# A selective scan with its kept state moved from the scan's start operand into the first column of its input

## The reference

```python
x = x + dilation_3x3(_gn(x))
x = x + mamba_block(_gn(x))
x = x + conv_3x3(_gn(x)) + bias
x = x + conv_3x3(_gn(x)) + bias
```

```python
def step(h, inputs):
    dt_t, x_t, B_t, C_t = inputs
    h = h * jnp.exp(dt_t[..., None] * A) + (dt_t * x_t)[..., None] * B_t[:, None, :]
    y = jnp.einsum('bds,bs->bd', h, C_t)
    return (h, y)
```

## Time and profile before

| | |
|---|---|
| median of 3 runs | 15620.45 us |
| the profiled execution | 15622.6 us, span 15620.4 us |
| DVE busy | 14588.6 us, 93% |
| POOL busy | 13980.9 us, 90% |
| PE busy | 12518.6 us, 80% |
| ACT busy | 8590.8 us, 55% |
| mean granted TensorE clock | 0.916 |

### The profile page before, as it was taken

One profiled execution on the slowest core, in us unless ns is written; L12 is line 12 of the kernel. 1 busy time (PEld: TensorE's weight loads), 2 busy tenths in 40 slices (PEclk: granted clock), 3 DMA queues, 4 the chain that ended last, 5 costly groups with the idle time before them and its releaser, 6 DMA issues.

```text
span 15620.4 us, 161058 instructions
## 1 busy us (share of the span) xinstructions
PE 12518.6 (80%) x26824; PEld 4912.5 (31%) x26824; DVE 14588.6 (93%) x13134; ACT 8590.8 (55%) x15334; POOL 13980.9 (90%) x6232
## 2 busy tenths in 40 slices
PE   4888878887887887878878788887888888788786
PEld 1333333333333333333333333333333333333332
DVE  6999999999999999999999999999999999999996
ACT  3555555555555555555555555555555555555553
POOL 5989989899898998989989898998989999899895
PEclk9999989999999898999999899999999999999898
DMA  3343433433434343343433434343343333434333
GB/s 95 103 115 107 109 114 102 122 103 106 116 104 120 100 109 115 105 118 104 110 115 105 117 103 116 107 109 114 102 122 103 106 117 105 120 101 109 116 103 84
DMA packets 1248863, 1701.30 MB, mean 109 GB/s; under 512 B 399212, under 2 KB 548148, under 8 KB 1245428
## 3 DMA queue, kind: packets, MB, share of 16 engines
q1 hardware_dynamic: 1247700, 1689.55, 38.6%
HBM read 1525.54 MB, written 124.13 MB: 106 GB/s over the span
## 4 chain that ended last, share of the span: by engine, by line
DVE 26%; issue 26%; POOL 20%; PE 19%; SPq 4%; DMA 3%; ACT 1%; DVEq 1%; POOLq 1%; ACTq 0%
POOL hc L646 15%; DVE h L1167 13%; PE y_ps L947 12%; DVE u_in L1151 8%; POOL u_in L621 3%; PE proj_ps L903 3%; DMA c_sb<-bc_dram 2%; SPq L431 1%; SPq L499 1%; PE b_ps L995 1%; PE side_ps L934 1%; DVE stats L1042 1%; PE side_ps L958 1%; DVEq L1165 1%; DVE norm L1122 1%
## 5 line engine op out<-in xcount | busy, mean ns | idle before, releaser
L646 POOL TENSOR_TENSOR hc<-h,c_sb 128x1024 f32<-128x1024 f32 x4096 | 9781.5, 2400 | 1182.8 <-DVE h L1167 696.7
L947 PE MATMUL y_ps<-hc,ident 128*128 128x512 f32 x16400 | 8584.4, 653 | 1013.0 <-POOL hc L646 1006.4
L1167 DVE TENSOR_TENSOR_SCAN h<-a_ps,carry,u_in 128x512 f32<-128x512 f32 x7168 | 8798.9, 1264 | 390.4 <-POOL hc L646 253.1
L751 ACT ACTIVATE a_ps<-dt,a_neg 128x512 f32<-128x512 f32 x8192 | 5605.2, 689 | 6147.0 <-DVE h L1167 6129.7
L947 PEld LDWEIGHTS y_ps<-hc,ident 128*128 128x128 f32 x16400 | 3276.4, 207 | 4849.4 <-issue 3119.9
L1151 DVE TENSOR_TENSOR u_in<-dtx,b_ps 128x1024 f32<-128x1024 f32 x2816 | 3364.0, 1195 | 142.1 <-PE b_ps L995 116.3
L621 POOL TENSOR_TENSOR u_in<-dtx,b_sb 128x1024 f32<-128x1024 f32 x1281 | 3088.3, 2411 | 0.1
L995 PE MATMUL b_ps<-b_parts,select 96*128 96x512 bf16 x2816 | 1156.0, 411 | 1493.6 <-DVE u_in L1151 1484.9
L1167 DVE TENSOR_TENSOR_SCAN h<-a_ps,u_in 128x512 f32<-128x512 f32 x1024 | 1205.5, 1204 | 208.9 <-POOL hc L646 184.4
L995 PEld LDWEIGHTS b_ps<-b_parts,select 96*128 96x128 bf16 x2816 | 283.5, 101 | 3104.2 <-DVE u_in L1151 2611.7
L958 PE MATMUL side_ps<-padded,w_main 128*128 128x512 f32 x1632 | 894.3, 634 | 154.2 <-DVE z L1134 71.7
(11 more groups left out here) (99 smaller groups left out, 6671.0 us busy)
## 6 DMA issues: line engine op xcount, KB each, us to landing
c_sb<-bc_dram SPq DMA_DIRECT2D x4100, 256.0 KB, 3.2
b_sb<-bc_dram SPq DMA_DIRECT2D x1283, 256.0 KB, 3.2
raw<-x SPq DMA_DIRECT2D x17, 2048.0 KB
x_dram<-vmax SPq DMA_DIRECT2D x68, 512.0 KB, 4.7
x<-x_dram SPq DMA_DIRECT2D x136, 256.0 KB, 8.0
z<-x_dram SPq DMA_DIRECT2D x68, 512.0 KB, 8.3
out<-raw SPq DMA_DIRECT2D x272, 128.0 KB
x_dram<-x SPq DMA_DIRECT2D x129, 256.0 KB, 3.8
```

Of the source, the lines that this page charges most:

```text
L646: pool.tensor_tensor(hc[:, ring_at(c * S + s, HC_RING)], h[:, ring_at(c * S + s, H_RING)], c_sb[:, s // C_GROUP % C_RING, s % C_GROUP:s % ...
L751: act.activation(a_ps[:, a_slot(c * S + s, half)], dt[:, c % 2, half], ACT.Exp, scale=a_neg[:, at:at + 1]).then_inc(a_made, 1)
L947: mm = pe.matmul(y_ps[:, half], ident[:, :], hc[:, ring_at((c * S + s) % (NC * S), HC_RING), half], start=False, stop=(s == S - 1), skip_g ...
L1167: dve.tensor_tensor_scan(h[:, r, half], a_ps[:, a_slot(c * S + s, half)], u_in[:, s % U_RING, half], start, ALU.mult, ALU.add).then_inc(h_ ...
```

## The change

All scans start from the constant zero. Since h[0] = a[0] h_kept + u[0], the same result comes out when a[0] h_kept is first added into column 0 of u_in. Three things are done for it.

1. At the start of each chunk but the first, ACT computes `first_a`, the decays of the chunk's first token for all 32 states (two activations of 128 x 32), after a wait for its own last decay.
2. Between the decay of half 0 and that of half 1 of every state of those chunks, ACT runs `add_carry`: two activations on one column, Identity with scale = carry and bias = u_in's first column, written in place. It waits for the product (u_in by DVE or by POOL), and signals `carried`, for which the scan of half 0 now waits instead of the product.
3. DVE makes its product two states ahead instead of one: in state s, between the two scans, that for s + 2. Two products stand ahead of the loop's body for an image instead of one. In PE's queue the place of the broadcasts is as before. The third place of the convolutions begins at state 29 instead of 28, and the mean and variance of one norm ("z1") move by one state.

```diff
-PLACES = ((15, 16, 19, 22), (24, 25, 26, 27), (28, 30, S + 2, S + 2))
+PLACES = ((15, 16, 19, 22), (24, 25, 26, 27), (29, 30, S + 2, S + 2))
...
-MEAN_AT = {"joint": (0, 23), "z1": (3, 29), "x1": (6, 24)}
-VAR_AT = {"joint": (0, 27), "z1": (4, 0), "x1": (6, 27)}
+MEAN_AT = {"joint": (0, 23), "z1": (3, 30), "x1": (6, 24)}
+VAR_AT = {"joint": (0, 27), "z1": (4, 1), "x1": (6, 27)}
...
+        first_a = sb("first_a", [P, NH, S])
...
             def make_decay(b, c, s):
                 if s == 0:
                     act.wait_ge(dt_done, chunk(b, c, NH))
+                    if c:
+                        act.wait_ge(a_made, state(b, c - 1, S - 1, NH))
+                        for half in range(NH):
+                            first = act.activation(first_a[:, half, :], a_neg[:, half * S:(half + 1) * S], ACT.Exp,
+                                                   scale=dt[:, c % 2, half, 0:1])
+                        first.then_inc(first_done, 1)
                 for half in range(NH):
 
                     act.wait_ge(h_done, a_free(b, c, s, half))
                     at = half * S + s
                     act.activation(a_ps[:, a_slot(c * S + s, half)], dt[:, c % 2, half], ACT.Exp,
                                    scale=a_neg[:, at:at + 1]).then_inc(a_made, 1)
+                    if c and half == 0:
+                        add_carry(b, c, s)
+
+            def add_carry(b, c, s):
+
+                if s == 0:
+                    act.wait_ge(first_done, first_chunk(b, c))
+                if s in DVE_U:
+                    act.wait_ge(u_made, made_by_vector(b, c, s))
+                else:
+                    act.wait_ge(pu_made, made_by_pool(b, pool_index(c, s)))
+                for half in range(NH):
+                    u0 = u_in[:, s % U_RING, half, 0:1]
+                    made = act.activation(u0, first_a[:, half, s:s + 1], ACT.Identity, bias=u0,
+                                          scale=carry[:, half, s:s + 1])
+                made.then_inc(carried, 1)
...
-                    if s in DVE_U:
+                    if c:
+                        dve.wait_ge(carried, carried_state(b, c, s))
+                    elif s in DVE_U:
                         dve.wait_ge(u_made, made_by_vector(b, c, s))
                     else:
                         dve.wait_ge(pu_made, made_by_pool(b, pool_index(c, s)))
                 dve.wait_ge(a_made, state(b, c, s, NH) - (NH - 1 - half))
-                start = carry[:, half, s:s + 1] if c else 0.0
-                dve.tensor_tensor_scan(h[:, r, half], a_ps[:, a_slot(c * S + s, half)], u_in[:, s % U_RING, half], start,
+                dve.tensor_tensor_scan(h[:, r, half], a_ps[:, a_slot(c * S + s, half)], u_in[:, s % U_RING, half], 0.0,
                                        ALU.mult, ALU.add).then_inc(h_done, 1)
...
-                if 0 in DVE_U:
-                    make_u(b, 0, 0)
+                for s in range(2):
+                    if s in DVE_U:
+                        make_u(b, 0, s)
...
-                        if (s + 1 < S or c + 1 < NC) and (s + 1) % S in DVE_U:
-                            make_u(b, *behind(c, s, -1))
+                        if (s + 2 < S or c + 1 < NC) and (s + 2) % S in DVE_U:
+                            make_u(b, *behind(c, s, -2))
```

More of the change, by code:

```diff
@@ L274, in build @@
         kept = sem("carry_kept")
+        first_done = sem("first_decays")
+        carried = sem("carry_in_first_input")
         hc_done = sem("hc_done")
@@ L334, in kept_state, with carried_state, first_chunk @@
             return b * ((NC - 1) * S) + (c * S + s + 1)
+        def carried_state(b, c, s):
+            return b * ((NC - 1) * S) + (c - 1) * S + s + 1
+        def first_chunk(b, c):
+            return b * (NC - 1) + c
         def behind(c, s, n):
```

## The result

The changed kernel takes 16056.36 us (median of 4 runs, 16051.36 to 16069.34), the kernel before beside it 15618.4 us: a ratio of 1.0283, interval [1.0265, 1.0301], slower by 438 us. I had forecast 15755, slower by 131. The sign and the mechanism stood in the forecast; its size did not.

What follows compares the result with a forecast made beforehand. DVE, busy 93%, was taken to set the pace, with PE closely behind. From 15622.6 us, - 430 + 134 + 24 + 224 + 32 + 115 + 32 = + 131 gave 15754, stated as 15755; range 15430 to 16080.

Steps and rivals of the forecast that it cites:

- Scans, 60 ns each, 296 us on the path: 7168 DVE scans lose their pointer operand, 60 ns each, 430 us in all; 296 us of it shortens the run.
- Products two ahead, 224 + 32 + 115 + 32 = 403 us: DVE waits for PE's broadcasts: 224 us up to state 17, 32 in first chunks, 115 and 32 in later states.
- the second place: Chunk 2, states 20 to 24, PE at half speed: scan (22, 0) 2.8 us late; 1.8 taken for four chunks.
- the first place: Chunk 5 of image 5, states 2 to 7, full clock: DVE waits 1.4 us for b_ps at product 7.
- The additions, 24 us: ACT's two per state fit its idle hole; only behind state 13's SiLUs they cost 0.5 us in three chunks.
- Rival 3: Where PE idles its clock falls to half speed, doubling the stalls: 16160, or 15960 for half of that; chance 0.10.
- Rival 1: PE keeps up, the broadcast for s + 2 is ready at the first scan of s: faster, 15400; chance 0.26.
- The signs that I named in advance: Profile after: scans near 1205 ns, DVE busy 400 us less, b_ps wait 400 or more, ACT near 68% busy.

Runs made afterwards that it cites:

- zero starts: Kernel before with 0.0 as the start of every scan and nothing added for the kept state: 15317.88 us, ratio 0.9807.
- 15438: Changed kernel with each broadcast into b_ps one state earlier in PE's queue: 15438.07 us, ratio 0.9887.
- 15320.11: Kernel before with products two states ahead, PE's broadcasts one state earlier, all scans from 0.0, no additions on ACT: 15320.11 us, ratio 0.9808.
- the move alone: Kernel before with products two states ahead and the three places moved, kept state as scan start, no additions: 16239.34 us, ratio 1.0401.
- the move and the lead: Kernel before with products two states ahead and PE's broadcasts one state earlier, kept state as scan start, no additions: 15555.6 us, ratio 0.9958.

## Why the prediction was wrong

The measured terms: zero starts - 297, the move without PE's lead 16056 - 15438 = 618 in the changed kernel (625 alone), the additions 118. Together + 439; measured, + 438. They are steps of one chain of kernels, so most of this closing is arithmetic. What it rests on is that 15320.11 and 15317.88 are the same, and that the move costs 625 us where nothing else is changed.

- **Scans, 60 ns each, 296 us on the path: right**, 297 measured. The size per scan is right. The share on the path is not shown by it: DVE's busy time fell by 518 us and its idle time grew by 219, against 430 and 134, and the two misses cancel.
- **Products two ahead, 224 + 32 + 115 + 32 = 403 us: the mechanism right, the size wrong**, 618. This is the step that failed, and in it the second place. For states 2 to 17 I had 256 us, and the two traces differ there by 258. Part of that is luck: state 5 alone has 237 and state 3, which was not on my list, 114, while states 7 and 2 get 95 and 56 back; and at the first place I had let PE's back-to-back queue shift as a whole (1.4 us; 1.98 in the rows, because u_ln was not there yet). For the other states I had 147 us, and the traces differ by 366 (the pair without additions, the move alone against the move and the lead, by 281 and 391). At the second place my bookkeeping at half the clock gave 2.8 us, near the 3.1 of the rows (4.81 + 0.90 - 1.91 - 0.73). I then took 1.8 for chunks 1 to 4, nearer to the full clock, where they cost 3.1 on average (197 us in 64 chunks). And I took 0.5 for the other chunks, which cost 2.6 (169 us in 64): product 23 waits in them, too (88 us in sum), and in chunk 0 so does the product made in state 31 (45 us). My upper bound, 2.9 in every chunk, was the measured size (366 us in 128 chunks).
- **The additions, 24 us: wrong**, 118, the second step that failed. The duration was nearly right (373 against 356), and in most states the hole between the decays does cover them. I had charged only the SiLUs in three chunks, and called the rest of ACT's chunk work covered. State 7, which I had at nothing, is 68 us longer in sum, state 14 is 81. The waits and decays at the chunk's start, priced at nothing, were not measured by themselves.
- **Rival 3, "the clock makes it worse": not as a change of the whole.** The mean granted clock went from 0.916 to 0.935. But DVE now waits for chains that run at half speed. At the second place they did so before the change, too (0.52). In front of the gate PE newly stands still, and the diagonal matmuls behind it take 1074 ns each in chunk 0 instead of 822 (713 instead of 692 over all chunks). My forecast had half speed in a rival and mostly full speed in the sum; it belonged into the sum. The measured 16056 lies between the two times of this rival, 15960 and 16160.
- **Rival 1** would have needed PE's 1484.9 us of waiting for products to be lead that could be used. They went, but 786 us of them into more waiting for hc (1006.4 to 1792.1), 295 into waiting for the split and 232 for the gate. Slack at one wait was not slack at the next one in the same queue. The sum of this rival doesn't match its words either: it says a third of the stalls and adds 50 us, where a third of 403 is 134; the low end, 15430, should have been 15461 (15622.6 - 296 + 134) before anything is added for ACT.
- The signs that I named in advance: scans at 1205 (1203), b_ps 400 us or more (1120.7), ACT busy 68% (65%), waits for decays under 250 us (68.6 for the additions, 4.8 for the decays alone). DVE's busy time fell by 296 us, not 400; see below.

## What to carry to other kernels

When an engine is made to produce further ahead, look at what feeds it: an in-order queue keeps its own distance, and each item asked for one step earlier has a whole step of foreign work in front of it. Move the supplier's item by the same distance in its queue as well; here that was one function and 618 us. And an operation put on a half idle engine is free only in the holes between two waits that it doesn't prolong: the same two activations, 0.65 us from start to end, cost 118 us between the decays and 433 more behind them.

## What the runs showed of the hardware

**Busy time is not work.** The scans' busy time fell by 458 us (10004.4 to 9546.5), DVE's as a whole by 296. 93 us of the difference is in the dilation's maxima on DVE, which read both operands from SBUF (four groups, 607 us instead of 514), 24 in the products. One of the four, before and after, with its spread (min/median/max ns):

```profile
L1122 DVE TENSOR_TENSOR norm<-norm,vmax x68: 1226/2102/2440, 75.1 to 15051.5; 128x1024 f32<-128x1024 f32 x68
```

```profile
L1155 DVE TENSOR_TENSOR norm<-norm,vmax x68: 1227/2544/2567, 74.2 to 15485.2; 128x1024 f32<-128x1024 f32 x68
```

It takes 1.23 us by itself and longer when a POOL instruction is under way. DVE and then POOL, at such a place in image 5 of the changed kernel:

```profile
5298.04 2.55 DVE L1155 TENSOR_TENSOR norm<-norm,vmax 128x1024 f32<-128x1024 f32 x1
```

```profile
5297.15 2.35 POOL L632 TENSOR_TENSOR u_in<-dtx,b_sb 128x1024 f32<-128x1024 f32 x1
5299.46 5.81 POOL L657 TENSOR_TENSOR hc<-h,c_sb 128x1024 f32<-128x1024 f32 x2
```

POOL's product is over at 5299.50, and DVE's maximum ends 1.09 us later, at 5300.59, as if it had only begun then. POOL's next two instructions take 5.81 us together, 1.1 more than two of 2.35. So each held off the other, and the profile counts both waits as busy time. The longest of the four kinds takes 3402 ns in the kernel before; it begins just behind the start of a POOL instruction. The median above moved with DVE's new phase against POOL. The scans, which read a_ps from PSUM and only one operand from SBUF, keep within 1159 to 1228 ns under the same POOL load. The Trainium skill ("SBUF — State Buffer", section "SBUF: two separate sides") says that a DVE instruction with two SBUF inputs and a GpSimd one that reads SBUF exclude each other for the whole instruction. The trace agrees, by the rows above.

**A pointer operand** costs 60 ns on a DVE scan (1264 to 1203) and about 90 on an activation of one column (373 for two, 190 without).

What stays open is how the 618 us divide between stalls at the full and at half the clock. I ran nothing that fixes the clock, and the sums by state don't separate them. The times by state come from one execution of each kernel.
